# Two heads on the two row halves of TensorE's array, and the maxima of both taken by one VectorE instruction

## The reference

```python
x = x + attn_a(layernorm(x), W_attn, W_proj)
x = x + ffn(layernorm(x), w1, b1, w2, b2)        # binarized weights
x = x + attn_b(layernorm(x), Wq, bq, Wk, bk, Wv, bv, Wo, bo, gamma, beta)
x = x + ffn(layernorm(x), w1, b1, w2, b2)

# both attentions: 16 heads of 16, T = 2048
att = jnp.einsum('bhqd,bhkd->bhqk', q, k) * (1.0 / math.sqrt(hd))
att = jnp.where(causal, att, -jnp.inf)
att = jax.nn.softmax(att, axis=-1)
att = att * decay_weight_matrix(T)               # attn_a only: zero from lag 511 on
y = jnp.einsum('bhqk,bhkd->bhqd', att, v)
```

## Time and profile before

| | us |
|---|---|
| median of three runs | 2740.55 (2735.39 to 2742.51) |
| the profiled execution | 2736.11 |
| its span in the trace | 2734.4 |
| granted TensorE clock over the span | 0.959 |
| PE, DVE, ACT, POOL busy | 2454.8, 1958.3, 1515.6, 1052.5 |

### The profile page before, as it was taken

One profiled execution on the slowest core, in us unless ns is written; L12 is line 12 of the kernel. 1 busy time (PEld: TensorE's weight loads), 2 busy tenths in 40 slices (PEclk: granted clock), 3 DMA queues, 4 the chain that ended last, 5 costly groups with the idle time before them and its releaser, 6 DMA issues. The chain is left out here.

```text
span 2734.4 us, 44488 instructions
## 1 busy us (share of the span) xinstructions
PE 2454.8 (90%) x13984; PEld 1404.0 (51%) x13984; DVE 1958.3 (72%) x4863; ACT 1515.6 (55%) x3309; POOL 1052.5 (38%) x1274
## 2 busy tenths in 40 slices
PE   4959999999999999969997599999999999997788
PEld 2535545454544545437774355555555555553676
DVE  5667787777787777716663588888888888870786
ACT  1218576776767685734332056666666666664333
POOL 0037777777777777751221301000101001011653
PEclk8969999999999999989998589999999999998999
DMA  4994142332505050033544751423505234102110
GB/s 134 252 144 63 24 56 36 44 51 32 70 11 75 13 69 6 5 114 77 125 96 98 111 75 16 64 38 44 70 15 72 32 51 62 18 7 99 47 54 31
DMA packets 181847, 171.03 MB, mean 63 GB/s; under 512 B 90352, under 2 KB 131056, under 8 KB 180848
## 3 DMA queue, kind: packets, MB, share of 16 engines
q1 hardware_dynamic: 181616, 168.18, 35.0%
HBM read 105.98 MB, written 61.08 MB: 61 GB/s over the span
## 5 line engine op out<-in xcount | busy, mean ns | idle before, releaser
L704 POOL TENSOR_TENSOR att_a_wd<-att_a_wt,decay 128x256 f32<-128x256 f32 (+3 forms) x896 | 754.6, 873 | 259.8 <-PE att_a_po L907 122.7
L742 ACT ACTIVATE att_b_wt<-att_b_ps 128x512 f32<-128x512 f32 (+3 forms) x1280 | 589.4, 539 | 354.6 <-PE att_b_ps L882 352.6
L782 DVE TENSOR_REDUCE att_a_mpart<-att_a_pm 128x1 f32<-128x512 f32 x768 | 513.5, 687 | 132.2 <-PE att_a_pm L860 129.0
L782 DVE TENSOR_REDUCE att_b_mpart<-att_b_pm 128x1 f32<-128x512 f32 x768 | 503.7, 686 | 109.7 <-PE att_b_pm L860 107.7
L860 PE MATMUL att_a_pm<-att_a_kop,att_a_qop 128*128 128x512 f32 (+3 forms) x1280 | 522.6, 426 | 55.6 <-DMA att_a_qop<-att_a_qop 28.2
L742 ACT ACTIVATE att_a_wt<-att_a_ps 128x512 f32<-128x512 f32 (+3 forms) x896 | 430.8, 506 | 218.1 <-PE att_a_ps L885 131.6
L860 PE MATMUL att_b_pm<-att_b_kop,att_b_qop 128*128 128x512 f32 (+3 forms) x1280 | 503.0, 408 | 36.6 <-DMA att_b_qop<-att_b_qop 29.9
L882 PE MATMUL att_b_ps<-att_b_qop,att_b_kop 128*128 128x512 f32 (+3 forms) x1280 | 453.2, 383 | 6.6 <-ACT att_b_wt L742 3.4
L722 POOL TENSOR_SCALAR_AFFINE_SELECT att_b_wt<-att_b_wt 128x512 f32<-128x512 f32 x128 | 81.6, 637 | 867.1 <-ACT att_b_wt L742 867.1
L860 PEld LDWEIGHTS att_a_pm<-att_a_kop,att_a_qop 128*128 128x128 f32 x1280 | 240.6, 193 | 324.6 <-DVE att_a_mpart L782 130.2
L860 PEld LDWEIGHTS att_b_pm<-att_b_kop,att_b_qop 128*128 128x128 f32 x1280 | 246.3, 194 | 277.1 <-DVE att_b_mpart L782 112.0
(11 more groups left out here) (174 smaller groups left out, 2622.6 us busy)
## 6 DMA issues: line engine op xcount, KB each, us to landing
att_a_kop<-qk SPq DMA_DIRECT2D x128, 128.0 KB, 7.7
att_a_qop<-qk SPq DMA_DIRECT2D x128, 128.0 KB, 8.0
att_b_kop<-qk SPq DMA_DIRECT2D x128, 128.0 KB, 6.2
att_b_qop<-qk SPq DMA_DIRECT2D x128, 128.0 KB, 6.8
qk<-qkv_a_qk_hi SPq DMA_DIRECT2D x32, 256.0 KB, 4.7
qk<-qkv_a_qk_lo SPq DMA_DIRECT2D x32, 256.0 KB, 4.5
qk<-mid_qk_hi SPq DMA_DIRECT2D x32, 256.0 KB, 4.0
qk<-mid_qk_lo SPq DMA_DIRECT2D x32, 256.0 KB, 4.5
```

The lines of the kernel that those rows point to most:

```text
L704: pool.tensor_tensor(wd[:, kq % 2, j, a:z], wt[:, kq % buffers, j, a:z], keep["decay"][:, u:u + z - a], ALU.mult).then_inc(w_decayed, 1)
L742: act.activation(wt[:, kq % buffers, j, a:CH], pe_[:, seen % EBANKS, 0:CH - a], ACT.Exp)\
L782: dve.tensor_reduce(mpart[:, c, piece, u:u + 1], pm[:, n % MBANKS, 0:w], AX.X, ALU.max, negate=True).then_inc(m_reduced, 1)
```

## The change

The four heads of a group become two pairs. Head j + 2a lies on row half a of the array (partitions 64a to 64a + 63, `rows(a)`); `kop` and `qop` hold two heads per column block instead of four. M matmuls are issued in pairs, one per row half, into two neighbouring banks. Off the diagonal one `tensor_reduce` reads both banks and writes both maxima; on the diagonal there are two instructions as before. S matmuls are issued in pairs too, into both S banks; each waits for the exponential of its own bank, and ACT takes the two exponentials one after the other. Row 64 is no longer free for the maxima: they go to a tile of their own, `mx` (one row per half, the rest zeros), and a further matmul with `ones_row` adds them. It is the last of its accumulation and carries the increment that ACT waits for. `mx` has one buffer, so SP waits for the older scores of that chunk before it writes. The mask on the diagonal of att_a becomes matmuls of 64 columns with constants `tri`, four per pair. Both attentions now have (4, 2) banks. The planner emits half as many S and M items, with the doubled cost for S and the single cost for M.

```diff
-            follow(number + 1, GH - 1, ("PV", c, kb))
+            follow(number + 1, 1, ("PV", c, kb))
...
-        for j in range(GH):
-            e.append((60.0 + CH - P * max(0, kb - TB * c), ("S", c, kb, j)))
+        for j in range(GH // 2):
+            e.append((2 * (60.0 + CH - P * max(0, kb - TB * c)), ("S", c, kb, j)))
...
-            follow((3, 0.0, ("MC", c)))
+            follow((2, 0.0, ("MC", c)))
...
-        kop = sb("kop", [P, 2, GH, T], F32R)
-        qop = sb("qop", [P, 2, NC, GH, CH], F32R)
+        kop = sb("kop", [P, 2, GH // 2, T], F32R)
+        qop = sb("qop", [P, 2, NC, GH // 2, CH], F32R)
+        mx = sb("mx", [P, NC, GH // 2, CH], F32R)
...
-        MBANKS, EBANKS = (4, 2) if decayed else (3, 3)
+        MBANKS, EBANKS = 4, 2
...
-        QK_LOADS = 16 * (2 * PAIRS + 1)
-        M_DMAS = 16 * (P // SQUARE)
+        QK_LOADS = 16 * 4 * PAIRS
+        M_DMAS = 16 * 2 * (P // SQUARE)
...
+                for a in range(2):
+                    heads = slice(head(0, a), head(0, a) + GH // 2)
+                    for r in range(PAIRS):
+                        part = slice(HALF * a + HD * r, HALF * a + HD * (r + 1))
+                        sp.dma_start(kop[part, par, :, cols].bitcast(F32), qk_g[g, r % 2, 1, :, heads, cols])\
+                          .then_inc(qk_in[par][c], 16)
+                        sp.dma_start(qop[part, par, c, :, :].bitcast(F32), qk_g[g, r // 2, 0, :, heads, cols])\
+                          .then_inc(qk_in[par][c], 16)
...
                         sp.wait_ge(mrow_ready, done(g + d, c))
-                        row = qop[MROW:MROW + 1, mpar, c, :, :].bitcast(F32)
-                        row = row.rearrange("o j (t k i) -> o (j t) k i", t=TB, k=P // SQUARE)
-                        for k in range(P // SQUARE):
-                            sp.dma_start(row[:, :, k, :], mrow[SQUARE * k:SQUARE * k + UNITS, c, :].bitcast(F32))\
-                              .then_inc(m_in[c], 16)
+                        if g + d > 0:
+                            sp.wait_ge(e_scores, scored(g + d - 1, c))
+                        else:
+                            sp.wait_ge(mx_zeroed, c + 1)
+                        for a in range(2):
+                            row = mx[HALF * a:HALF * a + 1, c, :, :].bitcast(F32)
+                            row = row.rearrange("o j (t k i) -> o (j t) k i", t=TB, k=P // SQUARE)
+                            for k in range(P // SQUARE):
+                                unit = SQUARE * k + TB * head(0, a)
+                                sp.dma_start(row[:, :, k, :], mrow[unit:unit + UNITS // 2, c, :].bitcast(F32))\
+                                  .then_inc(m_in[c], 16)
...
                         if piece < c:
-                            dve.tensor_reduce(mpart[:, c, piece, u:u + 1], pm[:, n % MBANKS, 0:w],
-                                              AX.X, ALU.max, negate=True).then_inc(m_reduced, 1)
-                        else:
+                            dve.wait_ge(m_scores, M_UNITS * (g + d) + n + 2)
+                            both = mpart[:, c, piece, :].rearrange("p (a u) -> p a u", a=2)[:, :, TB * j + qb]
+                            dve.tensor_reduce(both, pm[:, bank:bank + 2, 0:w], AX.X, ALU.max,
+                                              negate=True).then_inc(m_reduced, 2)
+                        for a in range(2 if piece == c else 0):
...
-                        mm = pe.matmul(pm[:, bank, 0:w], qop[:, mpar, c, j, qb * P:(qb + 1) * P],
-                                       kop[:, mpar, j, piece * CH:piece * CH + w], start=True, stop=True)
-                        mm.then_inc(m_scores, 1)
+                        for a in range(2):
+                            pe.wait_ge(m_reduced, M_UNITS * (g + d) + max(n + a + 1, MBANKS))
+                            if FARS:
+                                pe.wait_ge(f_done, FAR_UNITS * (g + d) + far_left(n + a) + MBANKS)
+                            mm = pe.matmul(pm[:, (n + a) % MBANKS, 0:w], qop[rows(a), mpar, c, j, qb * P:(qb + 1) * P],
+                                           kop[rows(a), mpar, j, piece * CH:piece * CH + w], start=True, stop=True)
+                            mm.then_inc(m_scores, 1)
...
+                        for a in range(2):
+                            pe.wait_ge(e_weights, E_UNITS * g + max(e + a + 1, EBANKS))
+                            pe.matmul(pe_[:, banks[a], 0:CH - z], kop[rows(a), par, j, kb * P:(kb + 1) * P],
+                                      qop[rows(a), par, c, j, z:CH], start=True, stop=False)
+                        for h in range(2 if decayed and kb >= TB * c else 0):
+                            for a in range(2):
+                                pe.matmul(pe_[:, banks[a], HALF * h:HALF * (h + 1)],
+                                          keep["tri"][rows(a), (0, 1, 2, 0)[2 * a + h], :],
+                                          keep["identr"][rows(a), rows(a)], start=False, stop=False)
+                        for a in range(2):
+                            mm = pe.matmul(pe_[:, banks[a], 0:CH - z], keep["ones_row"][rows(a), :],
+                                           mx[rows(a), c, j, z:CH], start=False, stop=True)
+                            mm.then_inc(e_scores, 1)
```

130 lines of the change are left out of this document (55 added, 75 removed).

## The result

The change makes the kernel slower: 3210.5 us median of four runs (3203.64 to 3215.13) against 2741.5, a ratio of 1.171 with a 95% interval of 1.168 to 1.174. The forecast had the sign and less than half of the size, +202 us where +469 were measured, and 3210 lies 100 us above its range. The span of the profiled execution is 3201.9 us, against 2734.4.

What follows compares the result with a forecast made beforehand. PE's own stream was taken to bound B where blocks are full. B +151, M's opening -2, A +51 and loads +2 gave +202 on 2736.1, 2938, as median about 2942; this case spans 2800 to 3080, the range 2725 to 3110.

Steps and rivals of the forecast that it cites:

- Row halves side by side, 0.23 us a pair: M matmuls in A and B: two on different row halves overlap, 0.23 us a pair, bounded by 0.23 and 0.46.
- Halves in series: Rival, chance 0.07: row halves do not overlap, B +380 and A +220, 3340 us.
- The pair's round trip, 1.73 us: S pairs on two banks: 1.73 us per full-width pair against 0.98 of ACT's work; 1.90 if mx waits for all QK.
- PE's lateness, 0.2 us in each of 28 full cells of B: Full cells of B: PV and an M pair make PE 0.2 us late for the next QK, 3.46 becoming 3.66.
- The transfer, +2.4 us a group of B: Maxima transfer, 8 DMAs per chunk instead of 4: +2.4 us once a group at chunk 3 of B.
- the rival with 0.05: Clock rival, chance 0.05: B falls to 1.2 GHz, a cell about 5 us, +300 more, 3240 us.
- A, +6 us a group: First attention (A): a group takes 130.5 us against 124.4, some +51 in all; bounds -85 to +140.
- DVE's pair instruction, worth nothing: One reduction over two banks, about 1.14 us against 1.20: 3 us per group, worth nothing since DVE waits.
- Two banks held at once cost nothing: M banks: DVE holding two with one instruction costs nothing while four banks make two pairs.
- Loads and opening: 16 load DMAs per chunk instead of 9: +1 us per attention, 0 to +4; M's opening gains some 2 in B.
- Tail of B, 3.46 us a cell: Last group of B, without M: 13 full cells go from 2.6 to 3.46 us, +11.
- its lower bound for B: B without PV's delay and the DMA wait: +9 us per group, +75 in all.

## Why the prediction was wrong

**Row halves side by side, 0.23 us a pair: right.** M's part of PE's busy time fell from 61.5 to 37.0 us a group. The Trainium skill (TensorE: Matmul & The Clock Gate, section "Measured speedup vs the span model") has a measured speedup of 3.07 for four row tiles. The timeline after agrees that row tiles run side by side: two in 0.23. "Halves in series" is out.

**The pair's round trip, 1.73 us: right to the hundredth.** 1.73 in the tail of the change, 1.74 where PV no longer disturbs it. The cause is shown by adding and taking away a bank: 2.6, 3.09, 3.13 and 3.60 us a cell in the tail. The Trainium skill (TensorEngine Tiling (Array Packing), section "PSUM Bottleneck") warns that tiling speeds up the matmuls and not the emptying of PSUM. B agrees: the round trip of two banks, 1.73 us, sets the pace there, and the 24.5 us less that M's matmuls are busy gained nothing.

**PE's lateness, 0.2 us in each of 28 full cells of B: the step that failed first.** The sum had 131.5 us for a group without the transfer, of which 125.9 were bare round trips (28 x 3.46 and 29 for the narrow cells) and 5.6 lateness. At a clock of 1.00 and without the transfer's wait the group takes 143.2: the lateness is 17.3 us, 0.43 us in each of 40 cells. It was undersized where I looked (3.83 against 3.66 in a full cell, since the M pair that stands between PV and QK counts in full) and left out of the narrow cells. By the starts of ACT's exponentials in such a group the 28 full cells take 108.0 us, where 102.5 were summed, and the twelve narrow ones 35.2, where 29 were; 2.7 us of this are three waits for DVE, and 1.1 one for POOL. The lateness missed is 12 us a group, about 90 of the 267 that were missing.

**The transfer, +2.4 us a group of B: right.** 2.27 and 2.3 in the rows. Without the wait the kernel was 36 us faster, the clock's share in it.

**The clock: the step that wasn't there.** The sum was made at full clock, and the rival with 0.05 had the wrong shape: it put all of B at 1.2 GHz, with cells of 5 us. In fact most full cells keep 2.4 GHz and two stretches a group don't: behind the wait for the transfer, and in the narrow cells of chunk 0. What was held against the rival, that the tail before kept 2.4 GHz with idle in each cell, is true of such cells and says nothing of these two stretches. In B that is worth 7.0 to 7.6 us a group by the groups above, some 58 us in eight. A has no group at full clock to read; at B's rate (7.3 us for 0.08) its 0.10 would be 9 us a group, 73 in all, which is an estimate. (Within the change A's own groups don't speak for less: 143.3 to 143.6 us at 0.90, 146.6 at 0.87.) Together about 130. That the rival's 3240 lies near the measured 3210 is chance.

**A, +6 us a group: wrong.** Measured +19 to +20. Some 9 are the clock's by that estimate. PE's waits for the far sums grew from 1.5 to 9.0 us, and shorter far sums gave 9 us of a group back, ACT's own work in it. I had let ACT pay 1.1 us for each pair of them and hadn't asked what they do to M: two heads of M now wait for two banks that ACT releases one after the other. That it is this order, and not ACT's work as such, is argued and not shown. The rows don't say what would be left with both repaired; neither was done without leaving work out or adding some.

**DVE's pair instruction, worth nothing: right** (1.225 us for one, as against 1.14 estimated; 21 us gained without it). "Two banks held at once cost nothing" held in B; ahead of B's first store it was wrong, by 14 us in the two profiles. **Loads and opening:** +10 us before the first store of y and +15 between A's last store and B's first, where 1 us, at most 4, was taken for each attention; not followed up.

**Tail of B, 3.46 us a cell:** 3.60, the lateness again. (A slip in the prediction, without effect: in its lower bound for B, +9 a group should read +10.7, which gives its +75.)

In sum, of the +469: 202 as forecast; about 90 from B's lateness in full clock; about 130 from the clock, of which A's part is an estimate; and some 45 that are left for A's waits and for the 25 us of the two openings.

## What to carry to other kernels

When two streams are made to share the array, count the PSUM banks before the matmuls: here the second half of a pair had to wait until its bank was read out, and the lost bank and the pairing each added half a microsecond to a cell of the tail. Then write down everything PE issues between the release of a bank and the matmul that refills it, in every kind of cell, and charge it in full. And where a change opens gaps in a stream that ran at full clock, forecast the time at both clock levels, since more than a quarter of the loss here, a share that is an estimate for A, had no waiting instruction to point at.

## What the runs showed of the hardware

- Two of four column strips of PV (x4 in the row) take 1.04 us, all four (x8) 1.05, and half the columns in all four 0.63. Cutting this group by strips saved nothing, and cutting it by columns did.
- The same instructions of B took 143.2 us at a mean granted clock of 1.00 and 150.2 to 150.8 at 0.92, in one execution. In the change the clock went to 0.51 for 10 us behind a wait of 2.27 us, and to 0.50 for 14 us in narrow cells where PE's rows are busy for 12.73 of 14.00. Without the wait for the transfer it was at 0.50 for 20 us in a group where PE's longest wait was 0.8 us.
- Eight more matmuls before that wait, and a few in chunk 0, made the kernel 26 us faster.
